# Queries and keys of the first tiles turned ahead of the scores, tile 0 loaded alone, and weights rounded ahead of the exponentials, in a gated attention and sparse-FFN kernel

## The chip, the cores and the metric

The kernel runs on one core of a Trainium2 chip. The metric is the device time of one execution in microseconds. The kernel before was timed three times: 750.56, 752.27 and 752.03 us, median 752.03 us.

The engines of the core are TensorE (PE; its weight loads are PEld), VectorE (DVE), ScalarE (ACT), GpSimd (POOL) and SyncE (SP, which here only issues DMAs). Each runs its own instructions in order; they meet at semaphores.

## The reference

`x` and `ctx` are 64 sequences of 128 tokens with 256 features. Per sequence:

```
q  = layernorm(x);  k = v = ctx                         # 16 heads of 16 features
a  = softmax(causal(q k^T / 4)) v
x2 = x + tanh(g_xattn) * a
xn = layernorm(x2)
p  = softmax(xn w_router + b_router)                    # 16 blocks of 64 hidden units
mask = the 4 blocks with the largest p
y  = (relu(xn w1^T + b1) masked by blocks) w2^T + b2    # hidden 1024
out = x2 + tanh(g_ffn) * y
```

All of it is in float32.

## The kernel before

A tile is one sequence, 128 tokens on the partitions. The whole program is one software pipeline: every engine walks the same iterations `i` from -4 to 71, and in each does the step of a different tile. With `N = 64` tiles, iteration `i` holds on TensorE, in this order: `scores(i+1)`, `q_transposed(i+2)`, `k_transposed(i+2)`, the first half of the FFN's hidden layer for an earlier pair (`hidden`, from `i = 5`) and of its output (`ffn_out`, from `i = 7`), the router's logits (every second iteration from `i = 4`), `attention_out(i-1)`, `shifted_scores(i)`, `x_transposed(i-2)`, the second halves, and `out_transposed(i-1)`. Iterations -4 to 4 thus have no FFN work.

The steps of the attention, with the lines of the profile:

- `normalised` (DVE, L541) writes the normalised queries into `q_pad`, where each head of 16 features takes 32 columns; `values` (POOL, L691) does the same for the context in `v_pad`. POOL computes the reciprocal deviation (`rstd_of`, L684 and L686).
- `q_transposed` (L240) and `k_transposed` (L251) turn them on TensorE, four transposes each, into PSUM banks `M1` and `M0`; ACT copies these to `qT` (L445) and `kT` (L449).
- `scores` (L273, the causal mask added by L283) fills four score banks; `row_maximum` (DVE, L548 and L550) reads them and puts the negated maxima of tile `b` into a spare column of the queries of tile `b+2`. They become a row when those queries are turned. After `q_copied` of tile `b+2`, SP moves that row with two small DMAs (`max_row`, L774) into `qT` of tile `b`. So the shift of tile `b` needs the turned queries of tile `b+2`.
- `shifted_scores` (L300) makes the scores again, transposed and with the maximum subtracted, into the same four banks; it waits for that DMA (`max_landed`) and for the maximum of tile `b+1` (`max_found`). `exponentials` (ACT, L454, two of 128x1024) reads them; `scores` of tile `b+2` waits for `exp_done` of tile `b`, since the banks are the same.
- `causal_weights` (POOL, L698) clears what lies above the diagonal, `attention_out` (L313) multiplies with the values into `M0`, ACT copies (L460), `out_transposed` (L328) turns into `M1`, and `attention_added` (DVE, L558 to L565, then L529 and L531) divides, adds the residual and takes the second layernorm's statistics.
- `x_transposed` (L339) turns the normalised result into `M0`; ACT copies it twice (`x_copies`, L466 and L469).

Matmuls of the FFN split each operand into a rounded high part and a rest. The weights are split at the start in eight pieces of 128x512: ACT rounds (`weights_high`, L492), POOL subtracts (`weights_low`, L712). Before the change, piece pairs are done in iterations -1, 0, 2 and 3, at the end of ACT's and POOL's iteration.

Banks 4 and 5 (`HID_BANK`, `OUT_BANK`) belong to the FFN and are unused until iterations 5 and 7. Loads are by pairs of tiles (`load`, L763 for the context, L767 for `x`), all from SP.

## Time and profile before

| what | value |
|---|---|
| time, median of 3 runs | 752.03 us (750.56 to 752.27) |
| the profiled execution's own time | 750.28 us |
| its span in the profile | 748.6 us |
| PE busy | 717.0 us, 96% |
| PE weight loads busy | 668.4 us, 89% |
| DVE busy | 505.2 us, 67% |
| POOL busy | 488.0 us, 65% |
| ACT busy | 430.8 us, 58% |
| share of PE in the chain that ended last | 92% |

The profiled execution took 1.7 us more than its span; what lies outside the span is start and end of the program. Times in the rows below are in microseconds from the start of the span. A busy PE is not a PE at its peak: matmuls are pipelined, and their modelled ends overlap the next ones.

### The profile page before, as it was taken

To read this page: it belongs to the slowest core of one execution; us is meant where nothing else is said; L and a number is where in the kernel's file an instruction comes from. 1 tells how busy PE (TensorE), PEld (TensorE's weight loads), DVE (VectorE), ACT (ScalarE), POOL (GpSimd) and SP (SyncE) were. 2 spreads that over 40 slices of the span, in tenths; PEclk is the share of its full clock that TensorE was granted. 3 is DMA by queue.
4 is the path that set the end of the run, shared out by engine and by line. 5 is a ranking of instruction groups with operands and counts; after the bars stand their busy time and mean duration, and the time that the engine had idled before them with its cause. 6 is when DMAs were issued, how large, how long until landed. Compare 5 with 4: busy or idle time off the path is not lost.

```text
span 748.6 us, 31053 instructions
## 1 busy us (share of the span) xinstructions
PE 717.0 (96%) x13512; PEld 668.4 (89%) x13512; DVE 505.2 (67%) x1428; ACT 430.8 (58%) x780; POOL 488.0 (65%) x663
## 2 busy tenths in 40 slices
PE   5669999999999999999999999999999999999888
PEld 4458999999999999999999999999999999999787
DVE  5468776776776676677677677667667767766552
ACT  3466566556556556656655655655665565565542
POOL 6587676676676667667667667666766766765542
PEclk9899999999999999999999999999999999999999
DMA  4312101111111111110111111011111011000010
GB/s 149 89 33 62 35 21 49 49 50 35 46 38 32 48 50 35 46 49 21 48 49 49 35 46 41 29 48 49 35 45 49 21 49 49 21 7 18 19 33 32
DMA packets 41397, 32.02 MB, mean 43 GB/s; under 512 B 15280, under 2 KB 41008, under 8 KB 41264
## 3 DMA queue, kind: packets, MB, share of 16 engines
q1 hardware_dynamic: 40992, 29.00, 13.0%
q8 instruction: 107, 1.75, 1.0%
q10 hardware_dynamic: 272, 1.05, 0.4%
q14 instruction: 26, 0.21, 0.1%
HBM read 19.03 MB, written 8.39 MB: 37 GB/s over the span
## 4 chain that ended last, share of the span: by engine, by line
PE 92%; ACT 3%; DMA 2%; DVE 1%; issue 1%; SPq 1%; POOLq 0%; POOL 0%; ACTq 0%
PE score_banks L300 10%; PE score_banks L273 9%; PE bank L380 8%; PE bank L401 8%; PE bank L403 8%; PE bank L402 8%; PE bank L382 8%; PE bank L381 7%; PE bank L313 7%; PE bank L240 5%; PE bank L328 3%; PE bank L251 3%; PE bank L339 3%; DMA qT<-qT 2%; PE score_banks L283 1%; ACT weights L454 1%
## 5 line engine op out<-in xcount | busy, mean ns | idle before, releaser
L698 POOL TENSOR_SCALAR_AFFINE_SELECT weights<-weights 128x1024 f32<-128x1024 f32 x128 | 138.0, 1103 | 150.2 <-ACT weights L454 150.2
L705 POOL TENSOR_TENSOR h_low<-hid,h_high 128x512 fp32r<-128x512 f32 x128 | 166.3, 1299 | 39.0 <-ACT hid L476 34.6
L603 DVE SCALAR_TENSOR_TENSOR hid<-bank,b_cols,used_all 128x256 f32<-128x256 f32 x248 | 108.1, 478 | 86.5 <-PE bank L382 84.3
L380 PE MATMUL bank<-xT_high,w_high 128*128 128x256 f32 x496 | 149.7, 302 | 0.0
L454 ACT ACTIVATE weights<-score_banks 128x1024 f32<-128x1024 f32 x128 | 124.3, 1023 | 38.9 <-PE score_banks L300 38.9
L401 PE MATMUL bank<-w_high,h_high 128*128 128x256 f32 x488 | 137.4, 281 | 3.2 <-DVE y_out L588 2.6
L382 PE MATMUL bank<-xT_high,w_low 128*128 128x256 f32 x496 | 139.4, 281 | 0.0
L381 PE MATMUL bank<-xT_low,w_high 128*128 128x256 f32 x496 | 139.0, 280 | 0.0
L403 PE MATMUL bank<-w_high,h_low 128*128 128x256 f32 x488 | 138.2, 283 | 0.0
L402 PE MATMUL bank<-w_low,h_high 128*128 128x256 f32 x488 | 137.9, 283 | 0.0
L460 ACT COPY oT<-bank 128x512 f32<-128x512 f32 x64 | 37.5, 586 | 115.1 <-PE bank L313 115.1
L401 PEld LDWEIGHTS bank<-w_high,h_high 128*128 128x128 f32 x488 | 92.2, 189 | 3.8 <-DVE y_out L588 3.0
L381 PEld LDWEIGHTS bank<-xT_low,w_high 128*128 128x128 f32 x496 | 94.0, 190 | 0.0
L380 PEld LDWEIGHTS bank<-xT_high,w_high 128*128 128x128 f32 x496 | 93.6, 189 | 0.1
L382 PEld LDWEIGHTS bank<-xT_high,w_low 128*128 128x128 f32 x496 | 93.2, 188 | 0.0
L403 PEld LDWEIGHTS bank<-w_high,h_low 128*128 128x128 f32 x488 | 92.0, 189 | 0.0
L402 PEld LDWEIGHTS bank<-w_low,h_high 128*128 128x128 f32 x488 | 91.8, 188 | 0.0
L475 ACT ACTIVATE h_high<-hid 128x512 fp32r<-128x512 f32 x128 | 82.7, 646 | 12.9 <-DVE hid L603 12.8
L548 DVE TENSOR_REDUCE q_pad<-score_banks 128x8 f32<-128x1024 f32 x64 | 77.8, 1216 | 10.9 <-PE score_banks L283 10.9
L686 POOL TENSOR_TENSOR rstd<-ve,half_power 128x1 f32<-128x1 f32 x128 | 77.5, 606 | 10.7
L476 ACT ACTIVATE hid<-hid 128x512 f32<-128x512 f32 x128 | 81.6, 638 | 0.0
L273 PEld LDWEIGHTS score_banks<-kT,qT 32*64 32x64 f32 x4096 | 63.5, 135 | 19.4 <-issue 17.2
(89 smaller groups left out, 1387.1 us busy)
## 6 DMA issues: line engine op xcount, KB each, us to landing
c_in<-in_ctx SPq DMA_DIRECT2D x32, 256.0 KB, 2.8
x_in<-in_x SPq DMA_DIRECT2D x32, 256.0 KB, 3.1
out_y<-y_out SPq DMA_DIRECT2D x31, 256.0 KB, 2.2
qT<-qT SPq DMA_DIRECT2D x128, 4.0 KB
w_stage<-in_w1T ACTq DMA_DIRECT2D x1, 1024.0 KB, 5.8
hid<-in_w2T SPq DMA_DIRECT2D x8, 128.0 KB, 2.7
used_all<-used SPq DMA_TRANSPOSE x32, 2.4
out_y<-y_out SPq DMA_DIRECT2D x2, 128.0 KB, 1.7
```

The source lines that it names most:

```text
L273: pe.matmul(out=score_banks[place_of, u, start:start + (1 + late) * HALF], lhsT=qT[rows, s, first + late * HALF:first + (1 + late) * HALF] ...
L380: pe.matmul(out=bank, lhsT=w1_high[:, k, c], rhs=high, start=k == 0, stop=False)
L381: pe.matmul(out=bank, lhsT=w1_high[:, k, c], rhs=low, start=False, stop=False)
L382: made = pe.matmul(out=bank, lhsT=w1_low[:, k, c], rhs=high, start=False, stop=k == KC - 1)
L401: pe.matmul(out=bank[:, 0:D], lhsT=high, rhs=w2_high[:, c, :], start=a, stop=False)
L402: pe.matmul(out=bank[:, 0:D], lhsT=high, rhs=w2_low[:, c, :], start=False, stop=False)
L403: made = pe.matmul(out=bank[:, 0:D], lhsT=low, rhs=w2_high[:, c, :], start=False, stop=z)
L454: act.activation(weights[:, b % 2, half * 2 * HB:(half + 1) * 2 * HB, :].rearrange("p h q -> p (h q)"), score_banks[:, 2 * half:2 * half + ...
L475: act.activation(h_high[:, p % 2, chunks], hid[:, n % 4], ACT.Relu)
L603: dve.scalar_tensor_tensor(hid[:, n % 4, j], hid_bank(n)[:, j * TOKS:(j + 1) * TOKS], b1_cols[:, c:c + 1], used_all[:, p % 2], ALU.add, AL ...
L698: pool.affine_select(out=w, in_=w, compare_op=ALU.is_ge, fill=0.0, base=0, pattern=[[0, 2 * HB], [1, S]], channel_multiplier=-1).then_inc( ...
L705: pool.tensor_tensor(h_low[:, p % 2, chunks], hid[:, n % 4], h_high[:, p % 2, chunks].bitcast(F32), ALU.subtract).then_inc(h_low_made, 1)
```

## The change

The changed kernel computes the same. In words:

- `q_transposed` of tiles 0 to 8 writes to `OUT_BANK`, `k_transposed` of tiles 0 to 6 to `HID_BANK`; later tiles use `M1` and `M0` as before. From iteration 0 on, these early transposes stand ahead of `scores(i+1)` in TensorE's order instead of behind it. In iterations -2 and -1 the keys go ahead of the queries.
- TensorE begins with 16 transposes of the identity, whose result nobody reads.
- Tile 0 of `x` and of the context is loaded by a DMA of its own, tile 1 by another; the first context loads are issued by ACT, those of `x` by SP.
- ACT begins with an exponential of one column and makes the four `tri` copies; DVE keeps the four `place` copies, in two pairs. POOL makes both masks ahead of `v_pad`. `q_pad` and `v_pad` are cleared only where no data will stand. `values(0)` stands ahead of the first `rstd_of`, the later ones of the start one iteration later.
- `weights_high` stands behind `k_evacuated` and ahead of `exponentials` in ACT's iteration; pieces go two each in iterations 0, 1 and 2, one each in 3 and 4. Pieces 0, 2 and 4 are subtracted on POOL, pieces 1, 3, 5, 6 and 7 on DVE, at the end of its iteration.
- The waits that guarded `M0` and `M1` are changed to fit.

```diff
 FFN_LAG = 5
+WARM = 16
 OUT_LAG = 7
...
+        def q_early(b):
+            return b < OUT_LAG + 2
+
+        def k_early(b):
+            return b < FFN_LAG + 2
+
+        def q_bank(b):
+            return banks[OUT_BANK if q_early(b) else M1]
+
+        def k_bank(b):
+            return banks[HID_BANK if k_early(b) else M0]
 
...
+            return {0: (0, 1), 1: (2, 3), 2: (4, 5), 3: (6,), 4: (7,)}.get(i, ())
+
+
+        W_LOW_BY_POOL = (0, 2, 4)
...
-                if b >= 4:
+                if not q_early(b):
                     pe.wait_ge(att_made, b - 3)
                 elif b >= 1:
                     pe.wait_ge(q_copied, b)
                 for r in range(HB):
-                    turned = pe.transpose(banks[M1][:, r * S:(r + 1) * S],
+                    turned = pe.transpose(q_bank(b)[:, r * S:(r + 1) * S],
...
-                if b >= 5:
+                if not k_early(b):
                     pe.wait_ge(xT_high_made, b - 4)
                 elif b >= 1:
                     pe.wait_ge(k_copied, b)
                 for r in range(HB):
-                    turned = pe.transpose(banks[M0][:, r * S:(r + 1) * S],
...
+                if b == 0:
+                    pe.wait_ge(place_made, U)
+                    pe.wait_ge(tri_made, U)
...
-                if b + 3 < N:
+                if b + 3 < N and not k_early(b + 3):
                     pe.wait_ge(k_copied, b + 4)
                 elif b >= 2:
                     pe.wait_ge(xT_high_made, b - 1)
+                elif b >= 1:
+                    pe.wait_ge(att_copied, b)
...
-                pe.wait_ge(q_copied, min(b + 4, N + MAX_LAG))
+                if not q_early(b + 3):
+                    pe.wait_ge(q_copied, min(b + 4, N + MAX_LAG))
                 if pr is not None:
                     pe.wait_ge(clipped_made, PAIR * (pr + 1))
-                if b + 3 >= N + MAX_LAG:
+                if b >= 1 and (q_early(b + 3) or b + 3 >= N + MAX_LAG):
                     pe.wait_ge(att_made, b)
...
-                pe.wait_ge(q_copied, min(i + 3, N + MAX_LAG))
-                if i + 3 > N + MAX_LAG:
+                if not q_early(i + 2):
+                    pe.wait_ge(q_copied, min(i + 3, N + MAX_LAG))
+                if q_early(i + 2) or i + 3 > N + MAX_LAG:
                     pe.wait_ge(att_made, min(i - 1, N))
...
-                    pe.wait_ge(w_low_made, 4)
+                    pe.wait_ge(k_copied, FFN_LAG + 2)
+                    pe.wait_ge(w_low_made, 2)
+                    pe.wait_ge(w_low_also_made, 2)
...
-                    pe.wait_ge(w_low_made, 8)
+                    pe.wait_ge(q_copied, OUT_LAG + 2)
+                    pe.wait_ge(w_low_made, 3)
+                    pe.wait_ge(w_low_also_made, 5)
...
 
+
             pe.wait_ge(ident_made, 1)
+            for n in range(WARM):
+                pe.transpose(banks[M0][:, 0:P], ident[:], ident[:])
             for i in ITERATIONS:
                 pr, pu = router_pair(i), used_pair(i)
                 p, m = hidden_pair(i)
                 out_b = out_tile(i)
-                if i + 1 == 0:
-                    pe.wait_ge(mask_made, 2 * U)
-                if 0 <= i + 1 < N:
-                    scores(i + 1)
-                if 0 <= i + 2 < N + MAX_LAG:
-                    q_transposed(i + 2)
-                if 0 <= i + 2 < N:
-                    k_transposed(i + 2)
+                if i < 0:
+                    if i + 1 == 0:
+                        scores(0)
+                    if i + 2 >= 0:
+                        k_transposed(i + 2)
+                        q_transposed(i + 2)
+                else:
+                    if q_early(i + 2):
+                        q_transposed(i + 2)
+                    if k_early(i + 2):
+                        k_transposed(i + 2)
+                    if i + 1 < N:
+                        scores(i + 1)
+                    if not q_early(i + 2) and i + 2 < N + MAX_LAG:
+                        q_transposed(i + 2)
+                    if not k_early(i + 2) and i + 2 < N:
+                        k_transposed(i + 2)
                 if p is not None:
                     hidden(p, m)
...
+            act.dma_start(c_in[:, 0, :], A_ctx[0]).then_inc(c_first_landed, 16)
+            act.dma_start(c_in[:, 1:PAIR, :], A_ctx[1:PAIR].rearrange("b p d -> p b d")).then_inc(c_landed[0], 16)
...
+            act.wait_ge(numbers_set, 2)
+            act.activation(scratch[:], half_power[:], ACT.Exp)
+            act.wait_ge(triangle_made, 1)
+            for u in range(U):
+                rows = slice(u * PAD, (u + 1) * PAD)
+                act.copy(tri[rows], triangle[rows, rows].unsqueeze(1).to_broadcast([PAD, HB, PAD])).then_inc(tri_made, 1)
             act.wait_ge(x_landed[1], 16)
             act.dma_start(w1_stage[:].rearrange("p k e c r -> p k (e c r)"),
                           A_w1T.rearrange("(k p) n -> p k n", p=P)).then_inc(w_landed[0], 16)
             for i in ITERATIONS:
                 pr, pu = router_pair(i), used_pair(i)
...
-                if 0 <= i + 2 < N + MAX_LAG:
+                if i < 0 <= i + 2:
+                    k_evacuated(i + 2)
                     q_evacuated(i + 2)
-                if 0 <= i + 2 < N:
-                    k_evacuated(i + 2)
+                elif i >= 0:
+                    if i + 2 < N + MAX_LAG:
+                        q_evacuated(i + 2)
+                    if i + 2 < N:
+                        k_evacuated(i + 2)
+                weights_high(i)
...
-                weights_high(i)
...
+            def weights_low(i):
+                for n in (n for n in pieces_of(i) if n not in W_LOW_BY_POOL):
+                    _w, stage, high, low = w_piece(n)
+                    dve.wait_ge(w_high_made, n + 1)
+                    dve.tensor_tensor(low, stage, high.bitcast(F32), ALU.subtract).then_inc(w_low_also_made, 1)
...
             dve.memset(minus_one[:], -1.0).then_inc(numbers_set, 1)
-            dve.memset(q_pad[:], 0.0).then_inc(q_zeroed, 1)
...
+                    dve.wait_ge(place_zeroed, 1)
+                    dve.wait_ge(ident16_made, 1)
+                    places(0)
+                    places(1)
                 if 0 <= i + 3 < N:
                     normalised(i + 3)
-                if i == -3:
-                    dve.wait_ge(place_zeroed, 1)
-                    dve.wait_ge(ident16_made, 1)
-                    dve.wait_ge(triangle_made, 1)
-                    for u in range(U):
-                        rows = slice(u * PAD, (u + 1) * PAD)
-                        dve.tensor_copy(place[rows].rearrange("p (j w) -> p j w", j=U)[:, :, 0:PAD],
-                                        ident16[rows, rows].unsqueeze(1).to_broadcast([PAD, U, PAD])).then_inc(mask_made, 1)
-                        dve.tensor_copy(tri[rows], triangle[rows, rows].unsqueeze(1).to_broadcast([PAD, HB, PAD])
-                                        ).then_inc(mask_made, 1)
+                if i == FIRST + 1:
+                    places(2)
+                    places(3)
                 if 0 <= i - 3 < N:
                     x_parts(i - 3)
                 if pr is not None:
                     route(pr)
...
-                for n in pieces_of(i):
+                for n in (n for n in pieces_of(i) if n in W_LOW_BY_POOL):
...
-            pool.memset(v_pad[:], 0.0).then_inc(v_zeroed, 1)
+            pool.memset(ident16[:], 0.0).then_inc(ident16_zeroed, 1)
+            pool.memset(triangle[:], 0.0).then_inc(triangle_zeroed, 1)
+            pool.wait_ge(ident16_zeroed, 1)
+            pool.affine_select(out=ident16[:], in_=ident16[:], compare_op=ALU.not_equal, fill=1.0,
+                               base=0, pattern=[[-1, P]], channel_multiplier=1).then_inc(ident16_made, 1)
+            pool.wait_ge(triangle_zeroed, 1)
+            pool.affine_select(out=triangle[:], in_=triangle[:], compare_op=ALU.is_ge, fill=NEG, base=0,
+                               pattern=[[-1, P]], channel_multiplier=1).then_inc(triangle_made, 1)
+            pool.memset(v_pad[:, :, :, HD:], 0.0).then_inc(v_zeroed, 1)
...
-                if 0 <= i + 3 < N:
+                if i == FIRST:
+                    values(0)
+                elif 0 < i + 3 < N:
                     values(i + 3)
...
-                if i == FIRST:
-                    pool.memset(ident16[:], 0.0).then_inc(ident16_zeroed, 1)
-                    pool.wait_ge(ident16_zeroed, 1)
-                    pool.affine_select(out=ident16[:], in_=ident16[:], compare_op=ALU.not_equal, fill=1.0,
-                                       base=0, pattern=[[-1, P]], channel_multiplier=1).then_inc(ident16_made, 1)
...
-            load(0)
-            load(1)
+            sync.dma_start(x_in[:, 0, :], A_x[0]).then_inc(x_first_landed, 16)
+            sync.dma_start(x_in[:, 1:PAIR, :], A_x[1:PAIR].rearrange("b p d -> p b d")).then_inc(x_landed[0], 16)
```

TensorE's order around the scores, iteration 1 of the kernel before (`scores` of tile 2 to `out_transposed` of tile 0; `q_pad` are queries, `v_pad` keys):

```order
27 L273 MATMUL score_banks<-kT,qT 64x128 [waits exp_done,k_copied,q_copied]
...
32 L283 MATMUL score_banks<-tri,place 64x2x2x32 x16
33 L240 MATMUL bank<-ident,q_pad 128x128 [waits q_copied,max_found,qn_made]
34 L240 MATMUL bank<-ident,q_pad 128x128 x3
35 L251 MATMUL bank<-ident,v_pad 128x128 [waits k_copied,v_made]
36 L251 MATMUL bank<-ident,v_pad 128x128 x3
37 L313 MATMUL bank<-weights,v_pad 32x128 [waits weighted,k_copied]
...
41 L300 MATMUL score_banks<-qT,kT 128x128 [waits max_found,max_landed1]
...
43 L328 MATMUL bank<-ident,oT 128x128 [waits q_copied,att_copied]
```

The same iteration of the changed kernel, whose lines are numbered anew (L262 queries, L273 keys, L295 and L308 scores, L340 attention, L325 shifted scores, L356 the output's transposes):

```order
30 L262 MATMUL bank<-ident,q_pad 128x128 [waits q_copied,max_found,qn_made]
31 L262 MATMUL bank<-ident,q_pad 128x128 x3
32 L273 MATMUL bank<-ident,v_pad 128x128 [waits k_copied,v_made]
33 L273 MATMUL bank<-ident,v_pad 128x128 x3
34 L295 MATMUL score_banks<-kT,qT 64x128 [waits exp_done,k_copied,q_copied]
...
39 L308 MATMUL score_banks<-tri,place 64x2x2x32 x16
40 L340 MATMUL bank<-weights,v_pad 32x128 [waits weighted]
...
44 L325 MATMUL score_banks<-qT,kT 128x128 [waits max_found,max_landed1]
...
46 L356 MATMUL bank<-ident,oT 128x128 [waits att_copied]
```

The eight transposes moved from behind the scores, which wait for `exp_done`, to ahead of them, and two waits for copies went.

On DVE, iteration 4 of the changed kernel, from the addition of tile 2 on (L615 and L617 are the row maximum, L640 the second normalisation, L608 the first, L646 the rest of `xT`, L662 the new subtraction of a weight piece):

```order
66 L625 RECIPROCAL gain<-bank 128x16 [waits att_turned]
67 L627 TENSOR_TENSOR att<-bank,gain 128x4x4x16 [waits recip_done]
68 L632 SCALAR_TENSOR_TENSOR x<-att,tanh_g,x_in 128x256 [waits att_made]
69 L593 BN_STATS stats<-x 128x6 [waits x2_made]
70 L595 BN_AGGR mv<-stats 128x2 [waits x2_stats]
71 L615 TENSOR_REDUCE q_pad<-score_banks 128x4x2 [waits scored]
...
77 L646 TENSOR_TENSOR xT_low<-xT,xT_high 128x2x128 [waits xT_high_made]
78 L685 MAX logit_top<-bank 128x8 [waits route_turned]
...
82 L697 MATCH_REPLACE marked<-found,clipped 128x16 [waits clipped_found] x2
83 L662 TENSOR_TENSOR w_low<-hid,w_high 128x512 [waits w_high_made]
84 L625 RECIPROCAL gain<-bank 128x16 [waits att_turned]
```

The subtraction at row 83 is new; nothing stood between the routing and the next tile's addition before.

## Rows read from the trace of the kernel before

**Rows 1.** The page's 40 equal slices of the span, PE's busy tenths.
```profile
PE   5669999999999999999999999999999999999888
```
**Rows 2.** Stretches: length, then PE, PEld, DVE, ACT, POOL busy (count), PEclk, DMA.
```profile
40.00:50.00 10.00, 6.13 (x218) 5.26 (x224) 7.76 (x15) 7.02 (x14) 9.34 (x12) 1.00 0.20 55
...
65.00:74.00 9.00, 8.74 (x195) 7.86 (x194) 8.73 (x26) 6.95 (x14) 7.96 (x11) 1.00 0.17 55
...
200.00:700.00 500.00, 499.10 (x9490) 467.54 (x9489) 345.95 (x989) 297.92 (x541) 328.88 (x442) 1.00 0.13 40
```
**Rows 3.** The chain that ended last, iterations 3 to 5: start, length, what.
```profile
41.04 1.02 PE score_banks L273 x45
...
42.28 0.60 PE bank L240 x4
...
42.90 0.59 ACT qT L445
...
43.51 0.60 SPq L774
...
44.15 1.67 DMA qT<-qT
...
45.87 1.22 PE score_banks L300 x32
...
47.11 1.95 ACT weights L454 x2
...
57.32 1.02 PE score_banks L273 x45
```
**Rows 4.** The same chain in iterations 0 and 1.
```profile
18.47 1.64 DMA qT<-qT
20.15 1.36 PE score_banks L300 x32
...
23.62 1.60 PE score_banks L273 x51
```
**Rows 5.** Timeline of the start: start, length, engine, line, operation, idle before.
```profile
1.47 2.23 POOL L718 MEMSET v_pad<- 128x2560 f32 x1
...
4.40 0.43 DVE L529 BATCH_NORM_STATS2 stats<-x_in 128x6 f32<-128x256 f32 x1 [1.67 <-DMA x_in<-in_x]
...
5.56 0.57 POOL L686 TENSOR_TENSOR rstd<-ve,half_power 128x1 f32<-128x1 f32 x1
...
6.73 1.08 PE L240 MATMUL bank<-ident,q_pad 128*128 128x128 f32 x4 [6.73 <-DVE q_pad L541]
...
7.07 1.28 ACT L445 ACT_TABLE_LOAD   x1 [7.07 <-DMA x_in<-in_x]
```
**Rows 6.** Two short stretches, columns as in rows 2.
```profile
26.50:27.00 0.50, 0.50 (x4) 0.50 (x3) 0.50 (x2) 0.38 (x1) 0.50 (x1) 0.50 0.00 0
...
28.00:28.50 0.50, 0.39 (x16) 0.39 (x20) 0.50 (x3) 0.06 (x1) 0.38 (x2) 1.00 0.01 2
```
**Rows 7.** Timeline of iterations 3 and 4, two lines: min/median/max ns, first to last start.
```profile
40.78 0.38 ACT L466 COPY xT<-bank 128x256 f32<-128x256 f32 x1
...
41.03 0.40 ACT L469 CAST xT_high<-bank 128x256 fp32r<-128x256 f32 x1
...
42.32 1.23 DVE L548 TENSOR_REDUCE q_pad<-score_banks 128x8 f32<-128x1024 f32 x1 [0.22 <-PE score_banks L283]
...
43.46 0.68 DVE L550 TENSOR_REDUCE q_pad<-score_banks 128x8 f32<-128x512 f32 x1
...
55.80 0.26 DVE L611 MAX8 logit_top<-bank 128x8 f32<-128x16 f32 x2
...
56.73 0.16 DVE L623 MATCH_REPLACE8 marked<-found,clipped 128x16 f32<-128x16 f32 x1
...
L712 POOL TENSOR_TENSOR w_low<-hid,w_high x4: 1267/1270/1280, 42.3 to 51.7; 128x512 fp32r<-128x512 f32 x4
...
L565 DVE SCALAR_TENSOR_TENSOR x<-att,tanh_g,x_in x64: 484/485/1483, 32.1 to 713.9; 128x256 f32<-128x256 f32 x64
```

More of the change, by code:

```diff
@@ L222, in pieces_of @@
         def pieces_of(i):
-            n = {-1: 0, 0: 2, 2: 4, 3: 6}.get(i, 8)
-            return range(n, n + 2) if n < 8 else ()
+            return {0: (0, 1), 1: (2, 3), 2: (4, 5), 3: (6,), 4: (7,)}.get(i, ())
+        W_LOW_BY_POOL = (0, 2, 4)
         block = ctx.enter_context(nc.Block())
@@ L250, in k_transposed @@
                 for r in range(HB):
-                    turned = pe.transpose(banks[M0][:, r * S:(r + 1) * S],
+                    turned = pe.transpose(k_bank(b)[:, r * S:(r + 1) * S],
                                           v_pad[:, b % VS, r * U:(r + 1) * U].rearrange("p h d -> p (h d)"), ident[:])
@@ L527, in _, with places @@
         def _(dve):
+            def places(u):
+                rows = slice(u * PAD, (u + 1) * PAD)
+                dve.tensor_copy(place[rows].rearrange("p (j w) -> p j w", j=U)[:, :, 0:PAD],
+                                ident16[rows, rows].unsqueeze(1).to_broadcast([PAD, U, PAD])).then_inc(place_made, 1)
             def stats_of(source, stats, mv, s, b, stats_made, mean_made):
@@ L689, in values @@
                 n, slot = divmod(landed(b), CS // PAIR)
-                pool.wait_ge(c_landed[slot], 16 * (n + 1))
+                if b == 0:
+                    pool.wait_ge(c_first_landed, 16)
+                else:
+                    pool.wait_ge(c_landed[slot], 16 * (n + 1))
                 pool.tensor_copy(v_pad[:, b % VS, :, 0:HD],
```

29 lines of the change are left out of this document (19 added, 10 removed).

## The prediction

> **What bounds the kernel now.** I read the page's slices first. TensorE is busy nine tenths or more from the fourth slice on, and in the first three it is at 5, 6 and 6 tenths [rows 1]. The stretches say the same: from 200 to 700 us PE is busy 499.10 of 500 us, with every other engine under 70%; from 40 to 50 us it is busy 6.13 of 10 us [rows 2]. So the main part is bound by TensorE's work, of which the change takes nothing away, and the start is bound by something else. What the start costs comes off the whole: all later work is a queue behind it.
>
> Then I read the chain of waits in the start. One iteration goes round through: scores, the queries' transposes, ACT's copy, SP's issue, the row's DMA, the shifted scores, the exponentials, and back to the scores, which wait for the exponentials' banks [rows 3]. From 41.04 to 57.32 us two rounds pass, 8.14 us each. Every link is serial only because the transposes of tile i+2 stand behind the scores of tile i+1 on TensorE. In iterations 0 and 1 the same links are longer: scores 1.60 us instead of 1.02, shifted scores 1.36 instead of 1.22 [rows 3, 4]. This is TensorE's lower clock: the granted clock is 0.50 (1.2 GHz) at 26.5 to 27.0 us and 1.00 (2.4 GHz) from 28.0 us on [rows 6]. The four transposes at 6.73 us took 1.08 us [rows 5], and at 42.28 us 0.60 us [rows 3], so the first microseconds ran at the low level too.
>
> **A round after the change, at the high clock.** Call E the end of the exponentials of tile i. The transposes of tile i+2 now run under them, so after E two paths run side by side.
> - Maximum: scores 42.32 - 41.04 = 1.28 us, both reductions 44.14 - 42.32 = 1.82 [rows 3, 7], 0.1 to start: with the 0.14 after E some 3.3 us.
> - Row: ACT's copy 0.61 (42.90 to 43.51), issue and DMA 45.87 - 43.51 = 2.36 [rows 3], and from iteration 3 on, ahead of the copy, the two x copies of the tile before, 0.65 (40.78 to 41.43) [rows 7]: 3.0 us, later 3.6.
> Then shifted scores, 1.24 (45.87 to 47.11), and exponentials, 1.95 [rows 3]. A round is 3.3 + 1.24 + 1.95 = 6.5 us, later 6.8. SP now has less time between two rows: in iteration 2 it also issues b1's columns and 512 KB of loads, which may sit before the next row; I put 0.1 us a round on it and keep 0 to 1 us for one of them. So two rounds of 6.5 to 6.6, then two of 6.9, where there were 9.3, 8.1, 8.1 and 8.1.
>
> **The first rounds.** The load of tile 0 alone brings x about 1 us earlier than 4.40 us [rows 5], but the queries need POOL's deviation too, and POOL is late: it clears `v_pad` (2.23 us at 1.47 [rows 5]) after making the masks, now half as many columns (1.1 to 1.4 us), and `values(0)`, 0.4 us, stands ahead of the deviation. I get the end of the deviation at 6.1 us, as before (5.56 + 0.57 [rows 5]). The early load is thus worth nothing for the queries. What helps: keys are turned during that wait, and ACT's table load (1.28 us at 7.07, in front of the first copy [rows 5]) is done by 2.5 us. The 16 transposes take 16 x 0.27 = 4.3 us at the low clock (a quarter of 1.08 [rows 5]), from about 1.55 to 5.9 us, and end just before the keys are wanted; they cost 0 to 0.6 us. First scores at 8.3 us. With 1.3 for them and 1.8 for the maximum the first maxima are there at 11.5 (four transposes and the copy of tile 1 fit beside). Statistics and normalisation of tile 2, 1.0 us, then queries and keys of tile 2, 1.2 us, scores of tile 1, 1.2, its maximum, 1.9: 16.9 us. The row is there at 12.5 + 0.6 + 0.6 + 2.4 = 16.1. So the first shifted scores start at 16.9 instead of 20.15 us [rows 4], and the scores of tile 2 at 16.9 + 1.2 + 1.95 + 0.14 = 20.2 instead of 23.62 [rows 4]: 3.4 us gained.
>
> This needs the high clock from about 8 us on. I take it: TensorE is then busy from 1.55 to 8 us almost without a gap, against 1.0 us out of the first 7.8 before, and no later pause is as long as the one that stood ahead of 20.15.
>
> The Trainium skill, page "TensorE: Matmul & The Clock Gate", section "Part 4: PE-mode transpose", says that transposes do not count as busy for the clock. By it the filler would heat nothing, and the low clock rival below would be the forecast. The trace does not bear it out here: the work just before the rise to 1.00, at 26.5 to 27.0 us, was transposes alone with PE busy the whole time [rows 6]; but scores stood ahead of them, so it is not settled.
>
> **The sum.** Start of the scores of tile 2: 3.4 us earlier. Scores of tile 4: two rounds of 13.1 us instead of 41.04 - 23.62 = 17.4 [rows 3, 4], 4.3 more. Scores of tile 6: 13.8 instead of 57.32 - 41.04 = 16.3 [rows 3], 2.5 more. Together 10.2 us, at 47.1 instead of 57.3 us.
>
> **What takes some back.** DVE gets five subtractions. POOL needs 1.27 us for one [rows 7]; on DVE a two-input operation of half the size takes 0.48 us at its least [rows 7], so 0.5 to 1.0 us, and I take 0.7. DVE's turn must be over before the next scores are: between two maxima it has 6.3 - 1.8 = 4.5 us of other work (7.76 of 10 us in a round of 8.14 [rows 2]) and 5.0 us of time in a round of 6.8, so in iterations 2 and 3 a piece costs 0 to 0.5 us. In iteration 4 the first routing (55.80 to 56.89, 1.1 us [rows 7]) and a piece stand in front of the addition of the next tile: DVE is then some 1.6 us late, of which the hidden layer, which starts in iteration 5, covers all but about 0.4. From 65 to 74 us DVE was already busy 8.73 of 9 us [rows 2], so a lag met there is not made up, and the 0.6 us of transposes that iteration 6 no longer has behind its scores gain 0.2 at most. Net loss 0.6. ACT's roundings (two of 128x512, no larger than its two copies before them) stand ahead of the exponentials, but between the end of a query copy and the exponentials ACT has 3.6 us (43.49 to 47.11 [rows 3]), of which the key copy takes 0.6: nothing, unless the weights land late. POOL loses five subtractions, 6.3 us, which the chain did not touch: nothing.
>
> The Trainium skill, page "SBUF — State Buffer", section "Who interferes with whom", says that a DVE instruction with two SBUF inputs and a GpSimd instruction that reads SBUF block each other for a whole instruction. This trace agrees: the two-input operation at L565 takes 0.484 us at the least and up to 1.483 [rows 7]. The subtractions are of this kind, so each may wait up to 1 us more.
>
> Gain 10.2 - 0.6 = 9.6 us. Against the profiled execution, 750.28 us (span 748.6), this is 740.7. The median of the runs shown is 1.75 us above that execution; I add 0.8 of it: **741.5 us**.
>
> **The rivals.**
> - *The clock stays low to about 17 us or later.* For: the two bursts before 18 us ran cold. Against: PE is busier now. Price: scores 0.7 us more three times, the transposes on the path 0.45 three times, shifted scores 0.14: 3.5 us. Time 745.
> - *The rounds are longer, DVE or the row's DMA being last.* For: DVE needs 6.3 us of a round without the piece and 7.0 with it; SP's loads are now closer to the rows. Against: the subtraction can run while POOL idles. Price: 0.7 us in each of four rounds, 2.8 us: 744.3.
> - *The transposes do not get under the exponentials*, because the normalised queries or the maxima are late. Against: DVE normalises 1.4 us after a maximum, the exponentials end 3.2 us after it. Then only the start's 3.4 us are left, less 0.6: 748.3.
> - *Slower: DVE becomes the chain in iterations 1 to 7.* Each of the five subtractions waits at its head for a rounding or is blocked by POOL, and with it the maximum on which the shifted scores wait. It decides from 10.2 / 5 = 2.0 us a piece; at 2.5 us, 12.5 us are lost: 752.6 by the profiled execution, 753.4 with my 0.8. Against: 0.7 plus 1.0 is the most that the rows show.
>
> **How the numbers follow.** Forecast 0.56 (739 to 743.5), low clock 0.15, longer rounds 0.20, transposes late 0.05, slower 0.04. The two middle cases reach to 746 or so, and part of them may add up; the bounds of the row's DMA, the filler and the pieces give 1.5 us down. Range 738.5 to 746.5. A measurement tells some 0.3%, 2.3 us, from no change: faster is below 749.8. Faster 0.93, same 0.03, slower 0.04.
>
> **What would show it.** In the changed profile: four transposes at 0.6 us and scores at 1.0 us from about 8 us on; the first shifted scores at 16.9 us; scores of tile 2 at 20.2, tile 4 at 33.3, tile 6 at 47.1 us, and query transposes starting before each exponential ends; first slices of PE at 7 to 9 tenths; 499 of 500 us busy in the middle; the DVE subtractions at 0.6 to 1 us. Wrong if the first full slice of PE is where it was, if the rounds stay at 8 us, or if a stretch behind 65 us has a PE gap that before had none.

## The result, and the profile after

The changed kernel took 742.19 us (median of 4 runs, 741.87 to 742.40), against 751.41 us for the kernel before in the same comparison: ratio 0.9877, 95% interval 0.986 to 0.9894, 9.2 us less. The profiled execution took 742.33 us, 7.95 us less than that of before, with a span of 740.5 us (8.1 less). A second set of four runs, taken later with other kernels, gave 742.19 us again (ratio 0.9881, 0.9863 to 0.9899); it was expected so:

> The changed kernel once more, to stand beside the other three on the same chip. Expected 742.2, within 1.5 us; where the granted clock falls in its first 25 us may differ from the first time.

The page's slices of PE after; the gain sits in the first three, as against [rows 1]:

```profile
PE   6889999999999999999999999999999999999888
```

The long middle (length, PE, PEld, DVE, ACT, POOL busy, granted clock, DMA) is as full as in [rows 2].

```profile
200.00:700.00 500.00, 498.11 (x9390) 466.81 (x9386) 345.40 (x980) 296.01 (x539) 330.46 (x443) 1.00 0.13 38
```

The start in order of time (start, length, engine, line, operation), to be laid beside [rows 5]: `v_pad` is half as long, the table load is over before the first copies of keys and queries, the statistics come 1 us earlier, but the queries' transposes only 0.46 us (6.27 against 6.73 us), since POOL's deviation ends at 5.76 us.

```profile
1.58 3.67 PE L443 MATMUL bank<-ident 128*128 128x128 f32 x16 [1.58 <-POOL ident L792]
...
2.22 1.28 ACT L544 ACT_TABLE_LOAD   x1 [2.22 <-issue]
2.31 1.17 POOL L802 MEMSET v_pad<- 128x1280 f32 x1
...
3.41 0.43 DVE L593 BATCH_NORM_STATS2 stats<-x_in 128x6 f32<-128x256 f32 x1 [1.21 <-DMA x_in<-in_x]
...
5.19 0.57 POOL L759 TENSOR_TENSOR rstd<-ve,half_power 128x1 f32<-128x1 f32 x1
...
6.27 0.66 PE L262 MATMUL bank<-ident,q_pad 128*128 128x128 f32 x4 [0.48 <-DVE q_pad L608]
```

The filler's 16 transposes took 3.67 us, not 16 x 0.27 = 4.3, but not because the clock was high. Each of them took 0.42 us (shortest, median and longest in ns below), as long as those of the kernel before at 6.73 us, and they overlap; the queries' four behind them took 0.27 us each, the duration at the high clock.

```profile
L443 PE MATMUL bank<-ident x16: 417/417/474, 1.6 to 4.8; 128*128 128x128 f32 x16
```

So the clock rose between the filler and 6.27 us. The chain of waits ahead of the first scores goes neither over the queries nor over POOL:

```profile
1.71 4.32 DMA x_in<-in_x
...
6.05 0.38 ACTq L550
...
6.48 0.58 ACT kT L494
7.06 0.50 ACT qT L490
...
7.60 1.05 PE score_banks L295 x50
```

ACT issues the load of w1 only when the load of `x` for tiles 2 and 3 has landed, and the first copies of keys and queries stand behind that issue. Here it cost next to nothing, since the queries' transposes ended at 6.93 us. In the second profile of the same kernel the issue came at 6.91 instead of 6.05 us, and the first scores at 8.51 us.

The clock did not stay high. The granted clock by short stretches, same columns:

```profile
10.00:11.00 1.00, 0.00 (x0) 0.00 (x0) 1.00 (x3) 0.55 (x2) 0.00 (x0) 1.00 0.94 354
11.00:12.00 1.00, 0.37 (x3) 0.38 (x4) 0.54 (x3) 0.00 (x0) 0.56 (x2) 1.00 1.00 384
12.00:13.00 1.00, 1.00 (x7) 0.73 (x5) 0.00 (x0) 0.58 (x1) 0.65 (x2) 0.58 0.91 329
...
21.00:22.00 1.00, 0.77 (x37) 0.80 (x40) 0.00 (x0) 1.00 (x4) 1.00 (x2) 0.50 0.00 0
22.00:23.00 1.00, 1.00 (x70) 0.93 (x58) 0.04 (x1) 1.00 (x3) 1.00 (x2) 0.80 0.07 20
```

TensorE stood idle from 9.9 to 11.6 us, waiting for the first maxima and the normalised queries of tile 2; the granted clock fell to 1.2 GHz between 12 and 13 us and came back after 22 us. The chain there, as against [rows 4], shows what it cost:

```profile
17.00 2.12 PE score_banks L325 x32
19.14 1.95 ACT weights L499 x2
...
21.23 1.51 PE score_banks L295 x57
```

The scores' starts against the forecast, from the timeline: tile 2 at 21.23 us (forecast 20.2, before 23.62), tile 3 at 28.43, tile 4 at 35.21 (33.3, before 41.04), tile 5 at 41.78, tile 6 at 48.79 (47.1, before 57.32). The rounds are 7.20, 6.78, 6.57 and 7.01 us. 8.5 us are gained at tile 6 and 8.4 at the maximum of tile 9; 8.1 arrive at the end.

In the warm rounds a link of [rows 3] is gone: the queries' transposes now run under the exponentials. From the timeline of iteration 3:

```profile
39.69 1.94 ACT L499 ACTIVATE weights<-score_banks 128x1024 f32<-128x1024 f32 x2 [1.47 <-PE score_banks L325]
...
40.70 0.66 PE L262 MATMUL bank<-ident,q_pad 128*128 128x128 f32 x4
...
41.78 0.98 PE L295 MATMUL score_banks<-kT,qT 32*64 32x128 f32 x51
```

### The profile page after: what moved, and what is told of

Same layout as the page of the kernel before. It is cut to its first block, busy times and chain, and to the rows that moved or that the text cites. A ratio compares the mean times of both kernels' runs of the same rounds, so it can differ in the third digit from the quotient of the medians.

```text
span 740.5 us, 31089 instructions
## 1 busy us (share of the span) xinstructions
PE 718.8 (97%) x13528; PEld 670.5 (91%) x13528; DVE 507.3 (69%) x1429; ACT 430.9 (58%) x785; POOL 481.9 (65%) x658
## 4 chain that ended last, share of the span: by engine, by line
PE 92%; DVE 3%; ACT 2%; POOL 2%; issue 1%; DMA 1%; SPq 0%; POOLq 0%; ACTq 0%
PE score_banks L325 9%; PE score_banks L295 8%; PE bank L411 8%; PE bank L436 8%; PE bank L435 8%; PE bank L434 8%; PE bank L413 8%; PE bank L340 8%; PE bank L412 8%; PE bank L262 5%; PE bank L356 4%; PE bank L273 3%; PE bank L367 3%; PE bank L381 1%; PE score_banks L308 1%
## 5 line engine op out<-in xcount | busy, mean ns | idle before, releaser
L615 DVE TENSOR_REDUCE q_pad<-score_banks 128x8 f32<-128x1024 f32 x64 | 77.8, 1215 | 9.8 <-PE score_banks L308 9.8
L325 PE MATMUL score_banks<-qT,kT 32*128 32x128 f32 x2048 | 76.0, 285 | 5.3 <-DVE q_pad L617 4.1
```

What stands on the lines that cost most here:

```text
L325: made = pe.matmul(out=score_banks[:, u, cols], lhsT=kT[rows, s, cols], rhs=qT[rows, s, cols], start=True, stop=True, tile_position=(u * P ...
```

## The experiments

Times are medians; each ratio is to the kernel before on the same chip. Milestones (start of the shifted scores of tile 5, where the FFN's work has begun) are from the profiled execution of each: 53.73 us in the changed kernel, 62.09 before. Rounds are given here from one start of the shifted scores to the next: 8.11, 6.78, 6.57 and 6.89 us in the changed kernel.

One thing limits the comparisons of e5, e6, e7 and e8 with the changed kernel. These four were timed together on one chip, and the changed kernel was not timed with them. From the maximum of tile 9 to that of tile 63, where all variants of the changed kernel do the same work, each of the four took 596.19 us in its profile, and the other seven profiles of the changed kernel and its variants 597.07 to 597.27. The difference builds up evenly over the tiles. What sets it no run shows. So by the profiles about 0.9 us of each such difference does not belong to the edit: it makes e6 and e8 look that much faster, and e5 and e7 that much less slow.

**The filler taken away** (e1)

```diff
-WARM = 16
+WARM = 0
```

> The changed kernel without the 16 transposes at TensorE's start. Theory A (the filler raises TensorE's clock for the first scores, and that shortens the start): transposes of tile 0 take 1.1 us instead of 0.66, the first scores 1.9 instead of 1.3, the first shifted scores start 0.5 to 1.5 us later than 17.0 us, and the time is 743 to 744. Theory B (the filler is worth nothing, because the clock falls again at 12 us and the long part of the low clock, 12 to 22.7 us, stays as it is or shifts forward): the first shifted scores within 0.5 us of 17.0 and the time within 0.6 us of 742.2.

745.28 us (742.07 to 746.30 over 5 runs; ratio 0.9925, 0.990 to 0.9949): 3.1 us slower than the changed kernel, and it varies by 4.2 us where the changed kernel varied by 1.0 over its eight runs. The profiled execution was the fastest of the five and no slower than the changed kernel: its first queries and scores ran at the low level (transposes 1.12 us), but the low stretch after that was shorter (granted clock 0.50 from 18 to about 21.5 us):

```profile
6.25 1.12 PE L262 MATMUL bank<-ident,q_pad 128*128 128x128 f32 x4
...
9.90 1.11 PE L273 MATMUL bank<-ident,v_pad 128*128 128x128 f32 x4
...
10.00 1.23 DVE L615 TENSOR_REDUCE q_pad<-score_banks 128x8 f32<-128x1024 f32 x1 [2.37 <-PE score_banks L308]
```

Theory A holds by the median, more than it said; theory B by the one profile. In which stretches the clock was low in the slower runs no trace shows.

**Transposes behind the scores again, rest as changed** (e2)

```diff
-                    if q_early(i + 2): q_transposed(i + 2)
-                    if k_early(i + 2): k_transposed(i + 2)
                     if i + 1 < N: scores(i + 1)
+                    if i + 2 < N + MAX_LAG: q_transposed(i + 2)
+                    if i + 2 < N: k_transposed(i + 2)
```

> The changed kernel with the transposes of tile i+2 again behind the scores of tile i+1 on TensorE, from iteration 0 on; banks, filler, loads and weights as in the changed kernel. Theory A (the place of the transposes is the main cause): rounds are again 8.1 us instead of 6.6 to 7.0, scores of tile 6 start 4 to 6 us later than 48.8 us, time 746.5 to 748.5. Theory B (the gain comes from the start: filler, loads, table, weights): rounds stay near 7 us and the time is 742 to 743.5.

749.47 us (10 runs; ratio 0.9979, 0.9959 to 1.0): nearly the whole gain is gone. Theory B falls. It is more than theory A said. The profiled execution, at 752.90 the slowest of the ten, has rounds of 10.22, 8.86, 9.58 and 8.12 us: only the last is theory A's 8.1, and the clock was low in two stretches (granted 0.50 from 8 to 28 us and from 38 to 45 us), with shifted scores of 2.13 us at 18.79 and 1.53 us at 37.87. The low clock is not the whole of it: the two runs whose mean granted clock was the 0.993 of the changed kernel's profile took 748.60 and 749.50 us, still 6.4 to 7.3 us more.

**The order alone, in the kernel before** (e3): early banks and transposes ahead of the scores, loads, masks, weights and TensorE's start untouched.

```diff
+                    if q_early(i + 2): q_transposed(i + 2)
+                    if k_early(i + 2): k_transposed(i + 2)
                     if i + 1 < N: scores(i + 1)
```

> The kernel before with only the early banks and the transposes ahead of the scores; loads, masks, weights and TensorE's start as before. Theory A: four rounds at 6.6 to 7.0 us instead of 8.1 to 9.3, start of the first shifted scores unchanged or later by up to 1 us because the transposes of tile 2 now stand ahead of the scores of tile 1 at the low clock: gain 5 to 6 us, time 745.5 to 746.5. Theory B: gain under 2 us, since ACT's weight roundings behind the exponentials now delay the copies of the next queries by 1.2 us a round: time 749.5 to 751.

748.58 us (10 runs; ratio 0.9954, 0.9935 to 0.9972): 2.9 us, half of what theory A said and outside both ranges. Its rounds are 7.16, 7.47, 7.62 and 7.60 us. The chain of waits goes over POOL and ACT's roundings (start, length, what):

```profile
23.29 1.02 ACT w_high L521 x2
...
24.42 0.48 ACT qT L474
...
37.09 2.32 POOL weights L727 x2
39.40 2.46 POOL w_low L741 x2
...
42.14 0.58 POOL rstd L715
...
42.74 0.81 DVE xn L602
```

The pair of roundings stands between the exponentials and the queries' copy, where before it was behind the transposes anyway; and POOL's two subtractions hold up the second deviation. So a round gains less than theory A said because the weights' work stands in the new path. That is one part. With these rounds the shifted scores of tile 4 come 4.0 us earlier than before (49.97 against 53.99); the next round then takes 10.91 us instead of 8.10 and leaves 1.2 us. In it POOL's second pair of subtractions holds the second normalisation until 50.79 us, and the granted clock is 0.50 from 52 to 58 us. How the 2.8 us divide between the two no run shows.

**First loads by pairs** (e4): `load(0)` and `load(1)` from SP again.

```diff
-            sync.dma_start(x_in[:, 0, :], A_x[0]).then_inc(x_first_landed, 16)
+            load(0)
+            load(1)
```

> The changed kernel with the first loads by pairs of tiles and all from SP, as before. Theory A (POOL's clearing and values bound the first queries, not the load): statistics start near 4.4 us instead of 3.41, the first queries' transposes 0.3 to 0.5 us later than 6.27 us, time 742.4 to 742.9. Theory B (the first tile's load bounds the start): everything 1.0 us later, time 743.2 or more.

743.92 us (4 runs; ratio 0.9902, 0.9878 to 0.9925). In the profile (743.12 us) the statistics start at 4.62 instead of 3.41 us and the transposes at 6.81 instead of 6.27:

```profile
4.62 0.43 DVE L590 BATCH_NORM_STATS2 stats<-x_in 128x6 f32<-128x256 f32 x1 [2.42 <-DMA x_in<-in_x]
...
5.74 0.57 POOL L756 TENSOR_TENSOR rstd<-ve,half_power 128x1 f32<-128x1 f32 x1
...
6.81 0.66 PE L262 MATMUL bank<-ident,q_pad 128*128 128x128 f32 x4 [0.70 <-DVE q_pad L605]
```

Of 1.2 us that the load is late, 0.54 reach the queries, a little more than theory A said; by the median, 1.7 us more, theory B is nearer. But the 0.54 us do not go on down the chain: the first scores, at 8.26 us, stand behind ACT's issue of w1's load (6.66 us), and the first shifted scores come at 16.74 us, no later than after. The 0.46 us that the shifted scores of tile 5 are late stem from a round of 9.03 instead of 8.38 us, in which the granted clock is 0.50 (from 47.5 to 51 us). The two runs at 743.0 and 743.1 us have a mean granted clock of 0.995, the two at 744.7 and 744.8 one of 0.989. So what the first load is worth by itself stays open.

**The weights as before** (e5): roundings behind the exponentials in iterations -1, 0, 2 and 3, all subtractions on POOL.

```diff
-            return {0: (0, 1), 1: (2, 3), 2: (4, 5), 3: (6,), 4: (7,)}.get(i, ())
+            return {-1: (0, 1), 0: (2, 3), 2: (4, 5), 3: (6, 7)}.get(i, ())
-        W_LOW_BY_POOL = (0, 2, 4)
+        W_LOW_BY_POOL = tuple(range(8))
```

> The changed kernel with the weights' pieces as before: rounding at the end of ACT's iteration (pairs in iterations -1, 0, 2, 3), all subtractions on POOL. Theory A (the early rounding matters because ACT would stop for the load of w1 or delay the queries' copies): the copy of the queries of tile 2 waits for the rounding of pieces 0 and 1, whose load lands at about 14.5 us, so it ends near 16 us instead of 12.9, and rounds with a pair are 1 us longer: scores of tile 6 start 3 to 5 us later than 48.8, time 745 to 747. Theory B (ACT has room, so the place of the roundings costs nothing): time within 0.6 us of 742.2.

746.32 us (5 runs; ratio 0.9919, 0.9885 to 0.9952), 4.1 us more. Theory B falls; A's size is right and its first half wrong. The load of w1 had landed at 12.48 us, and the queries' copy of tile 2 came at 13.53, 1.2 us later than after and without effect on the first shifted scores (17.05). The loss is in the rounds with pairs, 7.60 and 7.72 us. In the first a pair of roundings delays the queries' copy and with it the row:

```profile
35.45 1.17 ACT L535 CAST w_high<-hid 128x512 fp32r<-128x512 f32 x2
...
36.49 0.62 ACT L488 COPY qT<-bank 128x512 f32<-128x512 f32 x1
36.50 2.50 POOL L785 TENSOR_TENSOR w_low<-hid,w_high 128x512 fp32r<-128x512 f32 x2
...
39.48 1.17 PE L325 MATMUL score_banks<-qT,kT 32*128 32x128 f32 x32 [2.03 <-DMA qT<-qT]
```

In the second the shifted scores wait for the maximum instead, and the granted clock is 0.50 from 41 to 45 us. This profiled run took 743.71 us; it is 2.2 us behind the changed kernel at the shifted scores of tile 5 and at the maximum of tile 9. The 4.1 us of the median are more than that: two of the five runs took 742.83 and 743.71 us at a mean granted clock of 0.995 and 0.993, the other three 746.3 to 747.0 us at 0.991, 0.986 and 0.989. So part of the 4.1 us is low clock, which the longer pauses may bring; that they do is not shown.

**All subtractions on DVE** (e6) and **all on POOL** (e7), one number changed each (and the waits that count them):

```diff
-        W_LOW_BY_POOL = (0, 2, 4)
+        W_LOW_BY_POOL = ()                  # e7: tuple(range(8))
```

> The changed kernel with all eight subtractions on DVE, none on POOL. Theory A (POOL is on the chain in iterations 1 to 3: triangle, subtraction 1.25 us, deviation, then the second normalisation on DVE): the normalisations at 31.9 and 39.0 us come 1.2 us earlier, scores of tile 6 start 0.5 to 1.5 us earlier, time 741 to 741.8. Theory B (DVE is the fuller engine and three pieces more, 0.7 us each, fall on its path): 0.5 to 2 us slower, 742.7 to 744.

> The changed kernel with all eight subtractions on POOL, none on DVE. Theory A (POOL on the chain): two pieces, 2.5 us, stand between the triangle and the deviation in iterations 0 to 2, the normalisation waits 1.2 us longer in each of iterations 1, 2 and 3: 1.5 to 3.5 us slower, 743.7 to 745.7. Theory B (DVE is the bound and the five subtractions cost it 0.6 us or more): 0.5 us faster or the same.

e6: 740.34 us (4 runs; ratio 0.9849, 0.9818 to 0.988). e7: 743.51 us (4 runs; 0.9897, 0.9861 to 0.9933). The medians go as theory A said, e6 beyond its range and e7 a little short of it. The traces show the chain that A names. In the changed kernel the chain of waits goes over POOL's subtraction twice, at 29.77 and at 36.87 us; here the first:

```profile
27.44 2.32 POOL weights L774 x2
29.77 1.25 POOL w_low L788
...
31.89 0.81 DVE xn L640
```

In e6 no work of POOL stands in the chain between 23.6 and 47 us, and in e7 two subtractions, 2.48 us, stand at each of the two places instead of one. But the profile of e6 gives A little time: from the second round on its rounds are 6.79, 6.57 and 6.69 us against 6.78, 6.57 and 6.89 after, 0.2 us. Its first shifted scores start at 16.35 us, before any subtraction; that part is the clock, high until 17 us in this execution. Of the 1.85 us between the medians, 0.9 is the difference behind tile 9 named above. In e7 the third round took 8.62 us, and the clock was low again in part of it. DVE does not suffer either way, so the cover for DVE's subtractions was there.

**Fillers in the two pauses** (e8)

```diff
                         k_transposed(i + 2)
                         q_transposed(i + 2)
+                    if i == -1:
+                        filler(10)
 ...
                         scores(i + 1)
+                    if i == 0:
+                        filler(10)
```

> The changed kernel with ten more transposes of the identity behind the queries of tile 1 and ten behind the scores of tile 1, where TensorE waits from 9.9 to 11.6 us and from 15.0 to 17.0 us. Theory A (the low clock from 12 to 22.7 us follows from these pauses and lengthens the chain): the granted clock stays at 1.00, the shifted scores of tile 0 take 1.2 us instead of 2.1, scores of tiles 1 and 2 take 1.2 instead of 1.9, scores of tile 2 start 1.5 to 2.5 us earlier than 21.2, time 739.7 to 740.7. Theory B (transposes of the identity do not count as activity, or the low clock has another cause): granted clock 0.50 again from about 12 us and the time within 0.6 us of 742.2, or up to 1 us slower.

739.76 us (4 runs, 739.30 to 740.31; ratio 0.9842, 0.9805 to 0.9878): 2.4 us faster than the changed kernel by the medians. In the profile the maximum of tile 9 starts 1.9 us earlier than in the changed kernel (77.36 against 79.24; 1.2 earlier than in its second profile, 78.51), and 0.9 us come behind it. Theory B falls. Theory A holds but for one number: the granted clock reads 1.00 throughout, the shifted scores of tile 0 come at 16.54 us and are 1.2 us long, and the scores of tile 2 start at 19.85 instead of 21.23, 1.4 us earlier where it had said 1.5 to 2.5. The first scores started 0.5 us later than in the changed kernel (8.08 against 7.60), behind the issue of w1's load. From the first maximum to the scores of tile 4 it is 23.99 against 26.31 us: the low stretch cost 2.3 us.

```profile
12.00:22.00 10.00, 7.86 (x250) 6.85 (x250) 3.98 (x8) 6.25 (x11) 5.32 (x8) 1.00 0.44 134
22.00:40.00 18.00, 13.40 (x372) 11.24 (x370) 16.22 (x35) 11.81 (x20) 15.05 (x23) 1.00 0.24 63
```

```profile
16.54 1.21 PE score_banks L325 x32
...
17.77 1.95 ACT weights L506 x2
...
19.85 1.02 PE score_banks L295 x46
```

**Both** (e9: e8's fillers and e6's subtractions)

> The changed kernel with all eight subtractions on DVE and with the two fillers of ten transposes in the pauses of the start. Theory A (two separate causes, POOL's place on the chain and the low clock): the gains add in part, since the version with all subtractions on DVE also had less of the low clock; maximum of tile 9 starts at 76.5 to 77.3 us, time 738.5 to 739.7. Theory B (both versions gained by the clock alone): the same as with the fillers alone, 739.8.

741.13 us (4 runs, 741.02 to 741.57; ratio 0.9868, 0.985 to 0.9885): slower than either, a miss for both theories. In this execution w1's load is issued only at 7.00 us, TensorE is idle for 1.70 us ahead of the first scores (8.63 us), and the clock was low from 10 to about 13 us all the same. The ten transposes then take 1.97 us, against 1.26 in e8, and end at 13.62 us, 0.9 us after the queries of tile 2 are normalised (12.67), so they hold up what they were to bridge; the second maximum starts at 15.86 instead of 14.57 us. From the first shifted scores to those of tile 5 it takes 34.93 us against 35.32 in e8 (first rounds 6.56, 6.78, 6.60 and 7.25 against 6.72, 6.78, 6.57 and 7.52), so moving the last three subtractions to DVE is worth 0.4 us at most. At the maximum of tile 9 e9 is 0.9 us behind e8, and another 1.1 us come behind it, which is the difference named at the head of this section. Against the changed kernel on its own chip e9 is 1.1 us faster.

**The order behind, with fillers** (e10)

```diff
+                    if i == -1: filler(10)
 ...
+                    if i == 1: filler(10)
                     if i + 1 < N: scores(i + 1)
                     ...
+                    if i == 0: filler(10)
```

> The transposes behind the scores again, with three fillers of ten transposes (behind the queries of tile 1, ahead of the scores of tile 2, behind the keys of tile 2), so that the clock is high and only the order differs. Theory A (the order is the main cause by itself): rounds 8.1 us at the high clock, the first shifted scores near 17 us, scores of tile 6 near 53 us, time 744.5 to 746.5, some 5 us above the version with fillers and the transposes ahead. Theory B (the order mattered through the low clock that the longer pauses brought): 741 to 743.

748.58 us (9 runs; ratio 0.9963, 0.995 to 0.9977), 8.8 us above e8, and on its own chip 6.4 us above the changed kernel and 7.5 above e9. The rounds are 8.14, 8.82, 9.68 and 8.12 us. The clock was high until about 33 us and then fell, where no filler stands:

```profile
24.38 1.22 PE score_banks L325 x32
...
33.20 1.62 PE score_banks L325 x32
...
36.92 1.60 PE score_banks L295 x52
...
42.88 1.22 PE score_banks L325 x32
```

Two rounds at the high clock cost 8.1 us as theory A said, though the time is 2 us above its range; the shifted scores of tile 5 start 7.2 us later than in e8. Four rounds at 8.14 instead of 6.72, 6.78, 6.57 and 7.52 are 5.0 us of it. So theory A names the larger part. But theory B is not empty: the two longer rounds cost 2.2 us more. The first of them had a slower transfer of its row (2.35 against 1.66 us); the second is low clock (1.60 and 1.62 us instead of 1.02 and 1.22, and the transposes), behind a pause of 2.22 us ahead of the shifted scores at 33.20. That the order's longer pauses bring the low clock fits this, but is not shown by itself.

**Fillers alone, in the kernel before** (e11)

```diff
+            filler(24)                       # behind ident_made, into bank 5
             for i in ITERATIONS:
+                if i == 1: filler(12)        # ahead of scores(2)
 ...
+                if i == 0: filler(12)        # ahead of shifted_scores(0)
```

> The kernel before with fillers only: 24 transposes of the identity at TensorE's start, 12 behind the keys of tile 2, 12 ahead of the scores of tile 2, all into the FFN's output bank. Theory A: the clock is high from about 6 us, scores and transposes of tiles 0 to 2 each 0.4 to 0.7 us shorter on the path: maximum of tile 3 starts 2 to 3 us before 34.19 us and all behind it as much, time 748 to 749.5. Theory B: no rise before 20 us, time as before.

747.91 us (7 runs; ratio 0.995, 0.9931 to 0.9969): 3.3 us for instructions whose result nobody reads. The seven runs go by the mean granted clock: 746.24, 746.25 and 746.52 us at 1.00, 747.91 and 748.05 at 0.998, 748.76 and 748.90 at 0.995. The profile is of one of the first three. The maximum of tile 3 starts at 30.61 instead of 34.19 us, and the rounds stay at 8.1 to 8.2:

```profile
30.61 1.23 DVE L557 TENSOR_REDUCE q_pad<-score_banks 128x8 f32<-128x1024 f32 x1 [0.23 <-PE score_banks L283]
...
38.74 1.23 DVE L557 TENSOR_REDUCE q_pad<-score_banks 128x8 f32<-128x1024 f32 x1 [0.22 <-PE score_banks L283]
```

## Why the prediction was right, step by step

- *The start sets the gain, the rest is a queue behind it.* Right: the maximum of tile 9 starts 8.4 us earlier (79.24 against 87.61 us), and 8.1 us arrive at the end of the span.
- *The order shortens a round from 8.1 to 6.5 to 6.9 us.* Right: 6.78, 6.57 and 7.01 at the high clock; e10 gives the other side, 8.14. Which wait ends a round it had only in part: the new round was drawn with the maximum and the row, and what POOL loses was put at nothing because the old chain did not touch it. In the new one POOL's triangle, its subtraction and the deviation stand ahead of DVE's second normalisation, and so of the maximum. The price was small, 0.2 us by e6 and 0.4 by e9.
- *The early load is worth nothing for the queries, POOL is.* Nearly, for the queries: 0.54 us by the profile of e4. For the first scores both miss ACT's wait for the load of tiles 2 and 3, which the prediction did not draw; from one profile to another of the changed kernel and its variants they started between 7.60 and 8.63 us. The deviation ended at 5.76 us, not 6.1, as halving `v_pad` and the rest of POOL's start gave 0.35 us more than I had.
- *First scores at 8.3 us.* They came at 7.6, and yet the first shifted scores came at 17.00 us (forecast 16.9). Two errors met, and that is luck: the queries of tile 2 were turned at 11.63 us, 0.9 us before the forecast's 12.5, and the low clock took 1.0 us back between there and the shifted scores.
- *The clock is high from 8 us on.* This is the term that was mis-sized. It was high from the queries' transposes to 12 us, then low to 22 us. From the queries of tile 2 to the first shifted scores it took 5.37 us where I had 4.4; from there to the scores of tile 2 4.23 where I had 3.3; and the next round 7.20 where I had 6.5 and e8 has 6.73. That is 1.0, 0.9 and 0.5 us of low clock. The first was hidden by the better start; the later ones, with 0.1 us at the first shifted scores and some 0.2 us of the rounds themselves, are the difference between 10.2 and the 8.5 us gained at tile 6. I had said that no pause is as long as the one ahead of 20.15 us; that is so, and yet the clock fell behind a pause of 1.75 us. Nor was TensorE busy almost without a gap before 8 us: it was idle for 0.48 us ahead of 6.27 and for 0.68 us ahead of 7.60. e8 shows the term by itself: 2.3 us by its profile.
- *The number.* The profiled execution took 742.33 us where the sum gave 740.7, 1.6 us more. The forecast of 741.5 looks closer to the measured 742.19 because of the 0.8 us added for the median. That term was wrong for the changed kernel, whose profiled execution lies 0.1 us above the median of its four runs; it happened to point the right way.
- *The Trainium skill's rule, page "TensorE: Matmul & The Clock Gate", section "Part 4: PE-mode transpose", that transposes do not count for the clock.* The trace disagrees: nothing but transposes, the filler's 16 and the keys' four, stood ahead of the queries' transposes of 0.66 us at 6.27 us; without the filler (e1) these took 1.12 us at 6.25. And e11 had the high clock in its first scores (0.98 us at 9.71, against 1.62 at 9.61 before), with transposes alone ahead of them. The measurement decides: in this kernel they count.
- *DVE and the other losses take back 0.6 us.* Hardly: 0.2 us went between the scores of tile 6 and the maximum of tile 9. The other 0.3 us went evenly over the tiles behind (597.07 us from the maximum of tile 9 to that of tile 63 against 596.73 before), which the subtractions do not touch. A subtraction on DVE takes 0.68 us when nothing blocks it and 1.20 once, when POOL's triangle ran beside it:

```profile
L662 DVE TENSOR_TENSOR w_low<-hid,w_high x3: 682/684/1199, 33.5 to 48.1; 128x512 fp32r<-128x512 f32 x3
```

- *ACT's roundings are free ahead of the exponentials.* Right, but I had priced what they leave at nothing as well: e5 shows 2.2 us in the profile and 4.1 by the medians, part of it low clock, for the weights' whole handling, since behind the exponentials they would stand in front of the queries' copy. My sum had that in it only by drawing the new round without them.
- *The rivals.* The low clock rival happened in the larger part (2.3 of 3.5 us), but not as drawn: the clock was high first and low from 12 to 22 us. Longer rounds did not. Slower needed 2.0 us a subtraction; they cost 0.68 to 1.20.

## What to carry to other kernels

When a pipeline's main part is full, look at the round that fills it, draw which links are serial only because of an engine's order, and give the moved step a buffer that is idle in that phase. Removing one link shows the next at once: the order alone gave 2.9 us, and taking back the order from the finished version cost 7.3 (and fillers alone gave 3.3, taking back the weights' place cost 4.1, each with some low clock in it), so the parts of such a change cannot be added up from trials of one part. Read TensorE's clock in the fill phase, from durations as well as from the granted clock, and fill a short pause only with as much as fits into it at the low clock too: in e9 ten transposes took 1.97 instead of 1.26 us and held up the next step by 0.9.

## What had not been expected of the hardware

- A pause of 1.75 us (9.9 to 11.6 us) in a stretch that was else mostly busy was followed by 10 us at 1.2 GHz. A second profile of the same kernel had its low stretches elsewhere (granted clock 0.50 from 9 to 12 us, behind a pause of 1.58 us ahead of the first scores, and from 19 to 22 us); the milestones differed by up to 1.4 us and the time by 0.5 us. In e10 a pause of 1.51 us ahead of the first shifted scores was followed by no fall. Which pause is followed by one these runs do not settle.
- The granted clock is shown as 1.00 from the start of every profile to its first fall, while the first transposes take the low level's duration, 0.42 us each. In the kernel before it reads 1.00 until 21 us although the scores at 9.61 and 14.14 us took 1.62 and 1.59 us; in e8 it reads 1.00 to the end although four transposes at 6.27 us took 1.11. Before the first fall only the durations tell the level, and a mean granted clock leaves out what was low before it.
- Leaving the 16 transposes out made the time less steady: 742.07 to 746.30 us over five runs against 741.79 to 742.79 over eight.
